# Products with V of two cycles in one piece: 48 pieces in place of 80 in an attention kernel

## The reference, cut to what matters

```python
def attn(x, Wq, Wkv, Wo, bo):                  # x: 1 x 1024 x 512, 32 heads of 16, 8 key groups
    q, k, v = ...                              # 4 query heads share one group's k and v
    scores = einsum('bhqd,bhkd->bhqk', q, k)   # causal: -inf above the diagonal
    weights = softmax(scores / 4, axis=-1)
    ctx = einsum('bhqk,bhkd->bhqd', weights, v)
    return dot(ctx.reshape(b, t, d), Wo) + bo

def ffn(x, lora_A, lora_B, W, bias, lora_w):   # 8 LoRA pairs of rank 16, folded into W by the kernel
    return x @ W.T + bias + sum_n 2 * lora_w[n] * (x @ lora_A[n].T) @ lora_B[n].T

x = layernorm(x + attn(x, ...))
x = layernorm(x + ffn(x, ...))
```

## Time and profile before

| | us |
|---|---|
| median of 3 runs | 354.0 (352.69 to 354.79) |
| the profiled execution | 353.84 |
| its span | 352.00 |
| TensorE busy | 330.7 (94%) |
| VectorE busy | 267.8 (76%) |
| ScalarE busy | 221.6 (63%) |

### The profile page before, as it was taken

The page is one execution under the profiler, slowest core; times in us unless marked ns, Lnnn a source line. Parts: engine busy times, 40 slices in busy tenths (PEclk is TensorE's granted clock), DMA queues, the critical chain, the costliest instruction groups (busy, mean ns, idle before and its releaser), DMA issues.

```text
span 352.0 us, 7366 instructions
## 1 busy us (share of the span) xinstructions
PE 330.7 (94%) x2585; PEld 180.1 (51%) x2585; DVE 267.8 (76%) x844; ACT 221.6 (63%) x415; POOL 111.3 (32%) x193
## 2 busy tenths in 40 slices
PE   8889989999889999999999999999999999989992
PEld 4666545544444455444454454544545444547881
DVE  3438799889979999998989988899888961027663
ACT  4572366657647767776847858478586786852432
POOL 2373133355524345411222023120141112321553
PEclk9999999999989999999999999999999999999998
DMA  7969884353221111010010010000000000000002
GB/s 224 255 183 259 216 136 79 77 152 94 98 80 22 47 47 47 2 43 6 2 46 32 4 46 2 1 33 3 0 2 1 33 3 1 2 30 2 1 32 90
DMA packets 21317, 21.39 MB, mean 61 GB/s; under 512 B 6112, under 2 KB 17312, under 8 KB 21280
## 3 DMA queue, kind: packets, MB, share of 16 engines
q1 hardware_dynamic: 21280, 20.92, 22.4%
HBM read 14.68 MB, written 6.03 MB: 59 GB/s over the span
## 4 chain that ended last, share of the span: by engine, by line
PE 76%; DVE 9%; issue 5%; ACT 4%; DMA 2%; SPq 2%; POOL 1%; POOLq 0%; DVEq 0%; ACTq 0%
PE PS L1014 20%; PE PS L1156 18%; PE PS L992 17%; PE PS L1178 15%; DVE scrap L803 3%; PE PS L1084 2%; ACT PB L746 2%; PE PS L1076 2%; DMA TC<-in_L_attn_Wkv_dram 2%; PE PS L1060 1%; PE PS L1062 1%; DMA QS<-NMR 1%; DVE MX L796 1%; DVE MX L803 1%; DVE NM L819 1%
## 5 line engine op out<-in xcount | busy, mean ns | idle before, releaser
L746 ACT ACTIVATE PB<-PS 128x512 f32<-128x512 f32 x288 | 155.6, 601 | 60.9 <-PE PS L1178 59.2
L803 DVE CUSTOM_DVE_ANT_0 scrap<-PS,mask 128x128 bf16<-128x128 f32 (+3 forms) x256 | 111.1, 486 | 11.8 <-PE PS L992 10.6
L992 PE MATMUL PS<-KS,QS 96*128 96x512 bf16 (+3 forms) x384 | 108.4, 330 | 5.5 <-DVE MX L803 4.2
L1178 PE MATMUL PS<-QS,KS 99*128 99x512 bf16 x288 | 106.4, 383 | 0.3 <-ACT PB L746 0.3
L622 POOL TENSOR_SCALAR_AFFINE_SELECT PB<-PB 128x256 f32<-128x256 f32 (+1 forms) x96 | 46.4, 483 | 148.4 <-ACT PB L746 145.1
L796 DVE TENSOR_REDUCE MX<-PS 128x1 f32<-128x512 f32 x128 | 81.6, 683 | 9.9 <-PE PS L992 9.6
L1156 PE MATMUL PS<-PB,VX 128*32 128x256 f32 (+1 forms) x1280 | 79.5, 366 | 2.3 <-POOL PB L622 1.7
L992 PEld LDWEIGHTS PS<-KS,QS 96*128 96x128 bf16 x384 | 32.9, 98 | 56.2 <-DVE MX L803 15.1
L1156 PEld LDWEIGHTS PS<-PB,VX 128*32 128x32 f32 x1280 | 33.6, 109 | 41.6 <-issue 16.7
L1014 PE MATMUL PS<-XT,WQ 128*128 128x512 f32 x144 | 41.5, 420 | 2.0 <-DVE WQ L927 1.5
L1178 PEld LDWEIGHTS PS<-QS,KS 99*128 99x128 bf16 x288 | 27.4, 98 | 28.1 <-ACT PB L746 6.8
(11 more groups left out here) (76 smaller groups left out, 273.7 us busy)
## 6 DMA issues: line engine op xcount, KB each, us to landing
scr_q<-parts SPq DMA_DIRECT2D x8, 384.0 KB, 3.0
QS<-scr_q SPq DMA_DIRECT2D x16, 192.0 KB, 3.3
X<-in_L_attn_x_dram SPq DMA_DIRECT2D x8, 256.0 KB, 5.6
QS<-scr_q SPq DMA_DIRECT2D x16, 128.0 KB, 3.1
out_dram<-TC SPq DMA_DIRECT2D x8, 256.0 KB, 2.0
QS<-scr_q SPq DMA_DIRECT2D x16, 64.0 KB, 3.1
RAW<-in_L_attn_Wo_dram SPq DMA_DIRECT2D x1, 1024.0 KB, 6.1
RAW<-in_L_ffn_W_dram SPq DMA_DIRECT2D x2, 512.0 KB, 3.6
```

The costliest lines, as they stand in the source:

```text
L746: nc.scalar.activation(PB[:, cyc % NP_BUF, k, :], PS[:, score_bank(e), :], ACT.Exp, scale=SCALE)\
L803: last = nc.vector.tensor_tensor_reduce(out=scrap[:, n % 2, (j - j0) * width:(j - j0 + 1) * width], in0=bank[:, j - j0, :], in1=mask[:, HT ...
L992: last = nc.tensor.matmul(PS[:, CHUNK_BANK[n], k * width:(k + 1) * width], QS[0:ROWS, u % SLOTS, j, qb * P:(qb + 1) * P], KS[0:ROWS, g, k0 ...
L1178: nc.tensor.matmul(PS[:, score_bank(e), :], KS[0:NROW, u % G, kb * P:(kb + 1) * P], QS[0:NROW, u % SLOTS, heads[0]:heads[-1] + 1, s * HQ + ...
```

## The change

Pieces of V products move. `PV_BEHIND` says behind which cycle which pieces stand: the two cycles (p even, p odd) of a strip's pair go together behind the cycle after the second; a diagonal cycle with even p, which has no partner, goes alone as before. So from 80 pieces 48 are left: 16 with one cycle and 32 with two. A unit of the second half has them behind cycles 2 (0 and 1), 3 (2), 5 (3 and 4) and 7 (5 and 6), and none behind 1, 4 and 6; a unit of the first half has none behind its third cycle. The place of the turn of the maxima stays: behind cycles 4 and 11, where from unit 8 on no piece stands any more.

In the table of the fillers `T1a` goes from cycle 0 to 1 and `WO` from 7 to 8 (in the last block `T1a` 0 to 1, `T1b` 1 to 2). The plan of the maxima and of the banks is made from that table and moves with it: cycle 8 has eight chunks, cycle 9 one.

```diff
--- before.py
+++ after.py
@@ -70,6 +70,12 @@
     def last_of(u, s):
         return CYCLES.index((u, s, 2 * half_of(u) + s))
 
+
+    PV_BEHIND = {}
+    for c, (u, s, p) in enumerate(CYCLES):
+        if p % 2 or p == 2 * half_of(u) + s:
+            PV_BEHIND[c + 1] = [c - 1, c] if p % 2 else [c]
+
     LAST_OF = {last_of(u, s): (u, s) for u in range(NU) for s in range(2)}
 
     def heads_per_bank(width):
@@ -146,7 +152,7 @@
     FILL = dict(zip((2, 5, 8, 11, 13, 14, 17, 20, 22), LATER))
     for n, job in enumerate(STEPS):
         b, k = divmod(n, 6)
-        at = ((0, 2, 5, 7, 10, 13) if b < TB - 1 else (0, 1, 3, 6, 9, 11))[k]
+        at = ((1, 2, 5, 8, 10, 13) if b < TB - 1 else (1, 2, 3, 6, 9, 11))[k]
         FILL[FIRST[G] + BLOCK_CYCLES * b + at] = job
     assert len(FILL) == len(LATER + STEPS) and max(FILL) < NCYC - 2 and not set(FILL) & set(ROWS_AT)
     assert list(FILL) == sorted(FILL)
@@ -1191,11 +1197,12 @@
                     if j < len(pieces(cyc)):
                         piece_scores(cyc, j)
                     filler(cyc, j)
-                if cyc:
-                    accumulate(cyc - 1)
+                for c in PV_BEHIND.get(cyc, []):
+                    accumulate(c)
                 if cyc in ROWS_AT:
                     turn_maxima(ROWS_AT[cyc])
-            accumulate(NCYC - 1)
+            for c in PV_BEHIND[NCYC]:
+                accumulate(c)
 
 
             pe.wait_ge(max_read, len(CHUNKS))
```

## The result

| | before | changed |
|---|---|---|
| median us | 353.67 (352.69 to 354.79, 4 runs) | 363.12 (361.83 to 363.95, 4 runs) |
| ratio | | 1.0263 (95%: 1.0216 to 1.0309) |
| span of the profiled execution | 352.0 | 361.8 |

Slower by 2.6%, 9.45 us, where 6.0 us over the kernel before were forecast (359.8). The upper end of the range was 363.0, and the median of 363.12 lies 0.1 above it: the sign is right, the size is at the edge.

A forecast was written before the change was run, and what follows sets the result against it. TensorE's queue was taken as the second key half's bound, TensorE and VectorE by turns in the first. 353.84 - 2.5 (blocks) - 0.8 (d) - 0.7 (e) + 3.75 (a) + 3.2 (b) + 3.0 (c) = 359.8 us, range 354.2 to 363.0.

The forecast's parts named there:

- Switches: TensorE, between 32-column V products and 128-column neighbours: a pair of switches costs 0.208 us; 25 saved pairs give 5.2 us.
- (a): WO in cycle 8, T3 still in 10: T3 waits for the first norm, 1.25 us in three blocks, 3.75 in all.
- (b): T1a in cycle 1: T1b in 2 waits for VectorE's normalisation, 0.9 us in three blocks, 0.5 in the last.
- (c): Cycles without a piece: TensorE waits for maxima, 0.8 us in cycles 11 and 12, 0.2 in 4 and 5, per block.
- The block: Second key half, units 8 to 14: a block of 14 cycles should take 47.9 us in place of 45.6.
- (d): First key half: full switch gain 1.7 us, none 0, possibly another 1 lost to starved VectorE; half taken, -0.8.
- rival 3: One more meeting of small VectorE and GpSimd operations, with a clock fall: 2.4 + 1.5 us, total 363.7; chance 0.14.
- (e): Units 14 and 15: 1.0 us saved, 0.2 lost at the turn; 0.7 net, as ScalarE needs as long as TensorE.
- Rival 1: Whole kernel: TensorE never waits more than today, so only the switches are saved: 348.6 us; chance 0.08.
- rival 2: Second key half: only the fixed waits of T3 and T1b cost, 354.6 us or 355.8; chance 0.24.
- the forecast: Whole kernel: the sum of all terms, 359.8 us, slower, within 357.3 to 362; chance 0.54.

The follow-up runs named there:

- e6: The kernel before with 55 pieces of the second key half cut in two, same products: 365.57 us, ratio 1.0314.
- e9: The changed kernel with GpSimd's root ahead of its cycle's masks and ScalarE's first norm ahead of the first exponential: 361.94 us, ratio 1.0204.
- e1: The kernel before with the joins alone (48 pieces), table of fillers as before: 361.34 us, ratio 1.0208.
- e3: The changed kernel with T1a back in cycle 0 (last block T1a 0, T1b 1), WO still in 8: 364.83 us, ratio 1.0315.
- e4: The kernel before with 16 joins, only in the second key half and not strip 1's first two cycles, table as before: 356.11 us, ratio 1.0043.
- e11: The changed kernel with GpSimd's additions to X one cycle later in the first key half: 360.09 us, ratio 1.0177.
- e7: The kernel before with GpSimd's additions to X one cycle later in the first key half: 352.61 us, ratio 0.9949.
- e2: The kernel before with the new table of fillers alone, its pieces not joined: 365.69 us, ratio 1.0341.
- e5: e4 with T1a moved to cycle 1 and T1b to 3 (last block 1 and 2), WO still in 7: 352.05 us, ratio 0.9931.

## Why the prediction was right, and where it fell short

**Switches.** Forecast 0.208 a pair. e6 gives 0.21 to 0.22, the joined piece 1.87 (1.89 forecast), and the turn alone pays both ways (0.09 ahead, 0.10 behind). The number of pairs was one too high, 24 and not 25, since the pieces of cycles 78 and 79 already stood together: units 14 and 15 save four, not five.

**(a) T3.** Forecast 1.25, measured 1.37 in all three blocks; with the first score at 219.33, T3 follows it by 2.02 where 1.84 had been worked out, since the root ended at 220.36, 0.06 behind the time at which the norm could have started, and ScalarE's steps were a little longer. e9 confirms the chain. I had said that the fourth block would not have this wait; it has a smaller one (0.43 of idle time at 309.39). What failed there is "keeps WO in 6 and T3 in 9": the pieces around them moved. e1, which has the joins and the old table, has it too (0.59 from start to start).

**(b) T1b.** Forecast 0.9 in three blocks and 0.5 in the last; measured 0.86 and 0.52. Shown by the timeline and by e3, where it goes.

**(c) Cycles without a piece.** Forecast 0.8 in cycles 11 and 12; measured in block 1 0.23 at the turn, 0.28 at the first chunk behind it, and three chunks at 0.155, of which the kernel before had one: 0.82. Forecast 0.2 in cycles 4 and 5, measured 0.25. Right in place and size. e4, where strip 1's first piece stays single, has none of the waits at the turn and behind it, and one chunk at 0.16 as the kernel before.

**The block.** Adding up what TensorE's starts lie apart beyond the streaming time gives 5.34 us in block 1 of the kernel before and 8.06 in the changed one: 2.72, the whole of the 2.73 by which the block is longer. Forecast 2.3. The miss of 0.4 is 0.12 of (a), 0.07 of (c), less 0.04 of (b), and one step that failed: (b) names "a 0.2 wait for a chunk bank" in cycle 1, takes it off T1b's wait, and never adds it as a cost of its own. It measured 0.32, where the kernel before had 0.10. Over three blocks 7.8 us came where the terms sum to 6.95.

**(d) First key half.** Forecast -0.8, with 0 as "none". Where the clock does not fall, e11 against e7, it is 90.47 - 91.43 = -0.96, but 0.89 of that is the piece that the cut leaves to block 0: like for like there is next to no gain, -0.1. So the term failed: what eight pairs of switches saved is not in the time of this half. How it was lost is not shown, since the first four cycles alone vary between 14.1 and 15.8 us. In the changed kernel's own profile the half is +2.5, like for like +3.4: 1.7 of it in the first four cycles, where TensorE waits for queries, and 1.7 in cycles 4 to 23, which is rival 3, below.

**(e) Units 14 and 15.** The forecast was -0.7 (its own terms, 1.0 less 0.2, make 0.8) and, with T1b's 0.5, -0.2. Measured +0.4, and like for like, without the piece that the cut adds, -0.5. T1b's 0.52 and T3's 0.59 came, and a score waits 0.62 behind ScalarE where it waited 0.46; the kernel before had waits of 0.2 to 0.35 ahead of T2 and of three pieces that are gone. The step "ScalarE needs as long as TensorE there" is not so over this stretch: ScalarE is busy for 28.9 of 36.5 us in the kernel before, TensorE for 35.5.

**Rivals.** Rival 1 (348.6) and rival 2 (354.6 to 355.8) are excluded by the waits. What the change costs without either long meeting of VectorE and GpSimd is e11 against e7: 7.5 us by the medians, 7.3 by the spans, where the terms sum to 6.0. The difference of 1.3 is 0.8 in the blocks and 0.7 in (d), less 0.2 to 0.3 in (e). On top of that comes rival 3. Its mechanism is right: the joins bring VectorE's small operations and GpSimd's addition together a second time, in the changed kernel and in e1, e3 and e9. Its price of 2.4 + 1.5 was too high for the first part: the second meeting costs 0.4 in cycles 16 and 17 and the fall behind it 1.5 to 1.6, and the first meeting 1.0 and 1.4. The fall comes in two of the four profiles. In the profiles, moving the additions takes 4.8 us off the changed kernel's first key half and 1.4 off that of the kernel before, 3.4 more; but 1.2 of the 3.4 lies in the first four cycles, which the additions do not touch, and of the rest 1.5 to 2.0 goes with the second fall. By the medians the gain is 3.0 against 1.9, only 1.2 more, as fits an event that not every execution has. Both rival 3 and the forecast were true in part, and I had given them as alternatives; that the median came out within 0.1 of the upper end may in part be a matter of how often the clock fell. What the prediction could have looked up is the place of the small VectorE operations against GpSimd's additions in the first key half, which it shifts.

**What stays open.** In e1 to e3 the medians lie 1.7 to 3.2 us further above the kernel before than their stretches from cycle 0 to cycle 79 do, and their cycle 0 starts 1.3 to 2.3 us later than that of the kernel before. Nothing in the edits touches the start. In e2 a fall of the clock lies there, in e1 and e3 none does, and for them I did not find the cause; so differences of a microsecond among e1, e2 and e3 prove nothing, the waits do. Why the clock falls behind a stall in one execution and not behind the same stall in another stays open too.

## What to carry to other kernels

Before you move work together to save switches, list every fixed chain (a bank that another engine must empty, a norm ahead of an exponential) that the work covered where it stood, and price each with its cover gone: here a piece of 1.0 us covered four such places, and each join saved 0.2 us where a bare chain cost 0.24 to 1.1. Then move the fillers to the cycles that still have cover, and join only there (e5: 0.7% faster from the same joins that cost 0.4% in e4). And look for small VectorE operations beside GpSimd's additions whenever a change shifts time: one line was worth 1.9 us in e7 and 3.0 in e11, beside 2.4 for the joins of e5. Last, when you compare stretches of two orders, count what lies in each: here one piece on the other side of a cut turned a gain of 0.5 us into a loss of 0.4.

## What I had not expected of the hardware

A VectorE operation of 16 elements a partition, 0.17 us alone, took 1.20 us beside an addition of GpSimd. And the idle time of TensorE behind it does not tell whether the clock will fall. In the changed kernel 1.45 us of idle time came with a granted clock of 0.69 and 0.74 in the next 6 us. In e1, with the same instructions ahead and 1.44 us of idle time, it stayed at 1.00. In the kernel before 2.37 us of idle time came with 0.50 in the next 3 us; in e6, with the same order there, as long an idle time left the clock at its full level:

```profile
99.12 0.34 PE L992 MATMUL PS<-KS,QS 96*128 96x384 bf16 x1 [2.38 <-DVE MX L803]
```

```profile
99.00:102.00 3.00, 2.59 (x25) 1.22 (x25) 2.93 (x15) 2.28 (x5) 0.12 (x1) 1.00 0.33 108
```

So neither the length of the idle time nor the order of the instructions decides it here. The same order can have the fall in one execution and not in the next, so 1.4 us between two profiles can be the clock alone (12.22 against 10.83 us in cycles 13 and 14).
